# Causal attention by query tiles with streamed keys, and the feed of a finished tile run in half-tile steps between attention blocks

## The chip, the cores and the metric

The kernel runs on one core of one Trainium2 chip. The metric is the time of one execution on the device, in microseconds. The core has TensorE (PE in the profile), VectorE (DVE), ScalarE (ACT), GpSimd (POOL) and SyncE (SP), which here only issues DMAs. Each engine takes its instructions in the order of its own program, and the engines meet in semaphores. An instruction whose semaphore isn't there yet holds up all that stands behind it on its engine.

## The reference

One transformer layer on x of 4096 tokens by 256 channels, 16 heads of 16 channels. Cut to what matters (weights have a low-rank part that is folded in first):

```python
a = lora_linear(layernorm(x), w_attn, ...)            # to q, k, v
att = softmax(causal(q @ k.T / sqrt(16)))             # 16 heads, 4096 x 4096
x = x + layernorm(lora_linear(att @ v, w_proj, ...))
h = layernorm(x)
for blk in range(3):                                  # the feed
    y = qlora(h, 2*blk)                               # 256 -> 256
    y = gelu(layernorm(y) * gamma[blk] + beta[blk], approximate=False)
    h = qlora(y, 2*blk + 1) + h
x = x + layernorm(h)
```

## The kernel before

The program has stages, one after the other, each a block in which all engines start together: `prepare_weights`, `project` (q, k, v of all tokens; q and k go to DRAM in split parts, v stays on chip in `v_all`), `guard` (skipped here: it runs only where scores are large), `attend` and `feed`.

**attend.** The 4096 tokens are 8 tiles of 512. The outer loop (`Fori(0, NG)`, a hardware loop) runs over 4 groups of 4 heads. Its body is written out in full and goes through the query tiles from the last (j=7) to the first (j=0), and for each through its key blocks of 128: first the 4 blocks of the diagonal, with 512, 384, 256 and 128 queries left of 512, then the 4j full ones. That is 144 blocks a group, 576 in all, of which 128 are diagonal (32 sets of 4) and 448 full. For a block, `score` (L761) makes on PE the scores of 2 pairs of heads into `S`, which has 3 places of one pair. ACT takes the exp of each pair (L729) into `probs`, which has 6 places. POOL cuts the triangle in a diagonal block (L702). `weigh` (L779) multiplies the probabilities of four heads side by side with v into `O`, the last row of each head being the sum for the division. PE's order is score(b), weigh(b-2). `score` of pair n waits for the exp of pair n-3, which empties its place, and `weigh(b)` for both exps of b. At the end of a query tile DVE copies `O`, which has two places, into `acc` (L741, L745). Half of the tiles stay on chip, half go to DRAM. The q and k of the whole group (`q_op`, `k_op`) lie on chip. SP loads those of the next group tile by tile (L482, 8 DMAs for q of a tile and 8 for k), behind the tiles that no longer need them. In the first group ACT's queue issues 16 of the k loads.

**feed.** After all of attention it handles the tiles in 2 rounds of 4 at a time ("streams"), in an order that `orders()` works out from a table of durations. Per tile: the sums are turned by PE and divided (L946, L1043, L1044), projected (product L929), normalised and added to x, normalised again, and sent through three blocks of product, normalisation, turn (L922), gelu (L990), product, addition. The normalisation is shared: statistics on DVE (L100 to L110), the inverse root in 10 small steps on POOL (L80 to L90), the scaling on ACT (L977).

## Time and profile before

| what | us |
| --- | --- |
| median of 3 runs | 1530.82 (1530.27 to 1532.49) |
| profiled execution, its own time | 1532.92 |
| its span in the profile | 1531.2 |
| first matmul of attention, from the span's start | 177.29 |
| first matmul of each further head group | 435.99 and twice more, the last group's part ending near 1208 |
| feed | from there to the end |

The profiled execution is 1.7 us longer than its span, and 2.1 us longer than the median. The slices of the span show PE and ACT both at nine tenths or more through attention. In the feed ACT falls to about half and PE stays high. The rows themselves stand in a section of their own below.

### The profile page before, as it was taken

The numbers are of one execution on the slowest core, as the hardware profiler recorded it, in microseconds if no ns is written. First come the engines' busy times: TensorE is split into PE (matmuls) and PEld (weight loads), VectorE is DVE, ScalarE is ACT, GpSimd is POOL, SyncE is SP. The second block draws the span as 40 slices with busy tenths as digits, with TensorE's granted clock in tenths as the row PEclk, the third lists the DMA queues.
The fourth block names the chain that finished last, engine by engine and source line by source line (L and its number), as shares of the span: only waits on it lengthen the run. The fifth ranks groups of instructions, "written<-read, shape, count | busy, mean of one in ns | idle before, by whom it ended". The sixth has DMA issues, their size and how long they took to land. (4 is left out here: it accounts for less than half of the span.)

```text
span 1531.2 us, 27338 instructions
## 1 busy us (share of the span) xinstructions
PE 1415.8 (92%) x8838; PEld 621.7 (41%) x8838; DVE 319.3 (21%) x871; ACT 1218.0 (80%) x1552; POOL 315.9 (21%) x938
## 2 busy tenths in 40 slices
PE   6899499999989999998999998999999879997995
PEld 2455222222322223232223232222232558886784
DVE  3366100000000000000000000000000285578756
ACT  1366399999979999997999998999999555545644
POOL 0121100000120000021000012000010166446754
PEclk7699699999989999998999999999999999998998
...
GB/s 142 60 227 190 140 128 28 29 29 28 49 93 1 28 28 29 29 71 71 24 6 29 29 45 79 45 2 1 1 1 8 129 58 1 1 56 55 1 1 55
DMA packets 60327, 77.62 MB, mean 51 GB/s; under 512 B 16016, under 2 KB 31376, under 8 KB 60176
## 3 DMA queue, kind: packets, MB, share of 16 engines
...
## 5 line engine op out<-in xcount | busy, mean ns | idle before, releaser
L729 ACT ACTIVATE probs<-S 128x1024 f32<-128x1024 f32 (+3 forms) x1152 | 981.3, 1173 | 70.8 <-PE S L761 67.0
L779 PE MATMUL O<-probs,vg 128*32 128x512 f32 (+3 forms) x4608 | 578.8, 575 | 0.6 <-POOL probs L702 0.5
L761 PE MATMUL S<-q_op,k_op 64*128 64x512 f32 (+3 forms) x2304 | 502.4, 480 | 44.4 <-DMA k_op<-qk_rows 17.4
L761 PEld LDWEIGHTS S<-q_op,k_op 64*128 64x128 f32 x2304 | 213.7, 187 | 604.8 <-ACT probs L729 562.3
L702 POOL TENSOR_SCALAR_AFFINE_SELECT probs<-probs 128x256 f32<-128x256 f32 x256 | 102.7, 406 | 928.1 <-ACT probs L729 919.7
L929 PE MATMUL psC<-wfT,yTC 128*128 128x256 f32 x768 | 175.1, 386 | 7.9 <-ACT yTC L990 5.5
L741 DVE COPY acc<-O 128x512 f32 x16 | 11.1, 691 | 777.1 <-PE O L779 777.1
L929 PEld LDWEIGHTS psC<-wfT,yTC 128*128 128x128 f32 x768 | 146.6, 194 | 29.5 <-ACT yTC L990 7.1
L779 PEld LDWEIGHTS O<-probs,vg 128*32 128x32 f32 x4608 | 91.5, 108 | 138.6 <-issue 118.3
L977 ACT ACTIVATE yC<-uC,nmrC,rstdC 128x256 f32<-128x256 f32 x128 | 66.3, 590 | 56.4 <-POOL nmrC L93 56.3
L984 ACT COPY yTC<-psC 128x1024 f32<-128x1024 f32 x32 | 31.6, 1007 | 56.0 <-PE psC L922 56.0
L745 DVE COPY acc<-O 128x512 f32<-128x512 f32 x16 | 11.1, 691 | 248.9 <-PE O L779 248.9
L450 PE MATMUL psQ<-acc,wqkvT 128*128 128x512 f32 x128 | 59.9, 623 | 1.2 <-ACT acc L338 1.2
L1014 POOL TENSOR_TENSOR hbC<-hC,bffn 128x1024 f32<-128x1024 f32 x24 | 57.3, 2397 | 11.8 <-DVE hC L1036 10.6
L354 ACT ACTIVATE qf<-psQ,bqk 128x512 f32<-128x512 f32 x32 | 21.9, 684 | 34.7 <-PE psQ L450 34.2
L990 ACT ACTIVATE yTC<-psC,beta,gamma 128x512 f32<-128x512 f32 x48 | 34.3, 773 | 15.2 <-PE psC L922 15.2
L100 DVE BATCH_NORM_STATS2 stC<-uC 128x6 f32<-128x256 f32 x128 | 45.0, 414 | 1.1
L922 PE MATMUL psC<-ident,yC 128*128 128x128 f32 x256 | 34.4, 282 | 9.0 <-ACT yC L977 8.8
L450 PEld LDWEIGHTS psQ<-acc,wqkvT 128*128 128x128 f32 x128 | 24.8, 199 | 31.6 <-issue 31.6
L1036 DVE TENSOR_TENSOR uC<-psC,bffn 128x1024 f32<-128x1024 f32 x24 | 29.3, 1222 | 39.1 <-PE psC L929 39.1
L1036 DVE TENSOR_TENSOR hC<-psC,hbC 128x1024 f32<-128x1024 f32 x24 | 29.4, 1224 | 34.2 <-PE psC L929 34.0
L929 PE MATMUL psC<-wpT,yTC 128*128 128x256 f32 x128 | 30.9, 398 | 5.7 <-ACT yTC L984 5.7
...
## 6 DMA issues: line engine op xcount, KB each, us to landing
qk_rows<-parts SPq DMA_DIRECT2D x32, 512.0 KB, 3.1
q_op<-qk_rows SPq DMA_DIRECT2D x256, 64.0 KB, 2.3
k_op<-qk_rows SPq DMA_DIRECT2D x240, 64.0 KB, 2.3
...
xC<-in_L_attn_x SPq DMA_DIRECT2D x8, 512.0 KB, 4.8
...
out<-uC SPq DMA_DIRECT2D x8, 512.0 KB, 3.1
acc<-in_L_attn_x ACTq DMA_DIRECT2D x6, 512.0 KB, 4.7
```

Source lines behind the costliest of these rows:

```text
L100: last = nc.vector.bn_stats(st[:, b, :], src[:, b, :])
L450: last_mm = nc.tensor.matmul(psQ[:, m, :], g["wqkvT"][:, c, m * P:(m + 1) * P], xnT[:, u, c, :], start=(c == 0), stop=(c == NC - 1))
L702: nc.gpsimd.affine_select(out=tri, in_=tri, compare_op=ALU.is_ge, fill=0.0, base=0, pattern=[[0, 2], [1, P]], channel_multiplier=-1).then_ ...
L729: nc.scalar.activation(probs[:, pair % NP, :, 0:TT - q0], S[:, pair % NS, :, 0:TT - q0], ACT.Exp, scale=SCALE).then_inc(exp_ok, 1)
L761: last = nc.tensor.matmul(S[:, pair % NS, a, 0:TT - q0], k_op[mine, pair % 2, kb * P:(kb + 1) * P], q_op[mine, pair % 2, j * TT + q0:(j + ...
L779: last = nc.tensor.matmul(O[h * STRIP:(h + 1) * STRIP, o % 2, q0:TT], vg[:, kb, h, :], probs[:, (2 * b + h // 2) % NP, h % 2, 0:TT - q0], ...
L922: last = nc.tensor.transpose(ps[k][:, c * TT + b * P:c * TT + (b + 1) * P], src[:, b, c * P:(c + 1) * P], g["ident"][:, :])
L929: last = nc.tensor.matmul(ps[k][:, b * C:(b + 1) * C], yT[k][:, c, b * P:(b + 1) * P], w[:, c, :], start=(c == 0), stop=(c == NC - 1))
L977: last = nc.scalar.activation(dst[:, b, :], src[:, b, :], ACT.Identity, bias=nmr[k][:, b:b + 1], scale=rstd[k][:, b:b + 1])
L990: last = nc.scalar.activation(yT[k][:, c, :], ps[k][:, c * TT:(c + 1) * TT], ACT.Gelu, bias=g["beta"][:, col:col + 1], scale=g["gamma"][:, ...
L1014: nc.gpsimd.tensor_tensor(hb[k], h[k], repeated(g["bffn"][:, (2 * m + 1) * C:(2 * m + 2) * C]), ALU.add).then_inc(hb_ok[k], 1)
L1036: return nc.vector.tensor_tensor(dst, ps[k][:, :].rearrange("p (b c) -> p b c", b=NB), addend, ALU.add)
```

## The change

The loops of attention are turned round, and `attend` and `feed` become one stage, `attend_and_feed`.

- The outer order is now the query tile t from 0 to 7, and inside it the 4 head groups i. A pair (t, i) is a "visit", 32 in all. There is no hardware loop over groups: all 576 blocks are written out.
- q and k are no longer held for the whole group. Each visit loads its q tile (`q_op`, 3 places), and the k of each 512 keys that it goes through (a "chunk", `k_op`, 8 places). That is 144 chunk loads and 32 q loads of 8 DMAs each, all on SP, each set in a hardware loop of one turn (`Fori(0, 1)`). ACT issues none.
- v is written by `project` straight into the form that `weigh` reads, with the column of ones behind each head, so POOL's copies for each group go.
- `O` has one place. At a visit's end DVE turns it in 32x32 blocks into `o_turned`, divides, turns it back and SP moves the rows into `attT` (4 DMAs a visit). `acc`, its DRAM copy and PE's turning of the sums go.
- The feed of tile t runs in 22 steps on PE (11 steps for each half tile of 256 tokens), each between two blocks of attention: from block 26 + 76t on, about every 3.45 blocks, moved to a visit's end where one is near. All steps go through one PSUM place `F`, and each waits until DVE has emptied it for the step before. The steps of the last tile stand behind all blocks.
- The feed's normalisation is done by DVE alone (inverse root in dependent steps on 128x2 values, scaling too). ACT keeps the gelu, one call for both halves of a tile: 3 a tile, 21 of them between exps and 3 behind them all. The addition of h goes into the product's evacuation, for the last block into PE (4 more products with the identity).

`plan()` lays out all engines' orders with a table of durations when the kernel is built.

```diff
+VD = D + 1
+V_COLS = H * VD + STRIP - VD
...
+                    sp.dma_start(g["b2T"][:, m:m + 1], d["biases"][2 * (m // NC) + 1, at].rearrange("(p o) -> p o", o=1)).then_inc(small_in, 16)
...
-                    nc.gpsimd.memset(g["vg"][:, :, :, D:STRIP], 1.0).then_inc(ones_ok, 1)
-                    pool.wait_ge(ones_ok, 1)
+                    nc.gpsimd.memset(v_heads[:, :, :, D:VD], 1.0).then_inc(ones_ok, 1)
+                    nc.gpsimd.memset(g["vg"][:, :, H * VD:], 1.0).then_inc(ones_ok, 1)
...
-                    nc.vector.tensor_tensor(g["v_all"][:, bass.ds(n * NB, NB), :], psV[:, :, :],
-                                            g["bv"][:, :].unsqueeze(1).to_broadcast([P, NB, C]), ALU.add).then_inc(v_out, 1)
+                    for b in range(NB):
+                        last_v = nc.vector.tensor_tensor(v_heads[:, bass.ds(n * NB + b, 1), :, 0:D].rearrange("p o h e -> p (o h) e"),
+                                                         psV[:, b, :].rearrange("p (h e) -> p h e", e=D),
+                                                         g["bv"][:, :].rearrange("p (h e) -> p h e", e=D), ALU.add)
+                    last_v.then_inc(v_out, 1)
...
+HT = TT // 2
+HB = HT // P
...
+NS, NP = 3, 6
+RING, QS, AS = 8, 3, 3
+VISITS = [(t, i) for t in range(NT) for i in range(NG)]
+CHUNKS = [(v, s) for v, (t, i) in enumerate(VISITS) for s in range(t, -1, -1)]
...
+STEPS = ["project", "turn_x"] + [f"{x}{m}" for m in range(BLK) for x in ("first", "turn", "second")]
+FEED_FROM, FEED_EACH = 26.0, 76.0
...
+    for t in range(NT - 1):
+        for n, (name, k) in enumerate((name, k) for name in STEPS for k in range(2)):
+            at = FEED_FROM + FEED_EACH * (t + n / (2 * len(STEPS)))
+            near = min(boundary, key=lambda b: abs(b - at))
+            at = near if abs(near - at) < 1.7 else int(at)
+            steps.setdefault(at, []).append((name, t, k))
+    pe = []
+    for b in range(NBLK + LAG):
+        if b < NBLK:
+            pe.append(("score", b))
+        if b >= LAG:
+            pe.append(("weigh", b - LAG))
+        pe += steps.get(b, [])
+    pe += [(name, NT - 1, k) for name in STEPS for k in range(2)]
...
+                for x in order["SP"]:
+                    if x[0] == "k_load":
+                        c = x[1]
+                        v, s = CHUNKS[c]
+                        if c >= RING:
+                            sp.wait_ge(scored, 2 * CHUNK_END[c - RING] + 2)
+                        with sp.Fori(0, 1):
+                            load_rows(sp, d, k_op[:, c % RING, :, :], 1, VISITS[v][1], slice(s * TT, (s + 1) * TT), k_in[c % RING], LOW + need)
+                    elif x[0] == "q_load":
+                        v = x[1]
+                        t, i = VISITS[v]
+                        if v >= QS:
+                            sp.wait_ge(scored, 2 * LAST[v - QS] + 2)
+                        with sp.Fori(0, 1):
+                            load_rows(sp, d, q_op[:, v % QS, :, :], 0, i, slice(t * TT, (t + 1) * TT), q_in[v % QS], LOW + need)
...
+                        sp.wait_ge(o_ready, v + 1)
...
+                        for h in range(HG):
+                            row = (i * HG + h) * D
+                            sp.dma_start(attT[row % P:row % P + D, t % AS, row // P, :], o_div[h * STRIP:h * STRIP + D, v % 2, :]).then_inc(
+                                moved[v % 2], 16)
...
+                for _, n in order["POOL"]:
+                    pool.wait_ge(exp_ok, n + 1)
+                    tri = probs[:, n % NP, :, 0:P]
+                    nc.gpsimd.affine_select(out=tri, in_=tri, compare_op=ALU.is_ge, fill=0.0, base=0,
+                                            pattern=[[0, 2], [1, P]], channel_multiplier=-1).then_inc(cut_ok, 1)
...
-                with act.Fori(0, NG) as i:
-                    for b, (o, j, kb, q0) in enumerate(blocks):
...
+                for x in order["ACT"]:
+                    if x[0] == "exp":
...
+                    else:
+                        m, t = int(x[0][-1]), x[1]
+                        for k in range(2):
+                            act.wait_ge(dve_ok[k], done[f"copy{m}", t, k])
+                        for c in range(NC):
+                            col = m * NC + c
+                            last = nc.scalar.activation(zT[:, c, :], zT[:, c, :], ACT.Gelu, bias=g["beta"][:, col:col + 1],
+                                                        scale=g["gamma"][:, col:col + 1])
+                        last.then_inc(gelu_ok, 1)
...
+                def score(b):
+                    v, t, c, kb, q0 = BLOCKS[b]
+                    if b == 0 or BLOCKS[b - 1][0] != v:
+                        pe.wait_ge(q_in[v % QS], LOAD * (v // QS + 1))
+                    if kb % NB == 0:
+                        pe.wait_ge(k_in[c % RING], LOAD * (c // RING + 1))
+                    for n in (2 * b, 2 * b + 1):
+                        if n >= NS:
+                            pe.wait_ge(exp_ok, n - NS + 1)
...
+                def weigh(b):
+                    v, t, c, kb, q0 = BLOCKS[b]
+                    i = VISITS[v][1]
+                    first = kb == t * NB
+                    if first and v:
+                        pe.wait_ge(o_out, v)
...
+                    if b in DIAG:
+                        pe.wait_ge(cut_ok, cuts[2 * b + 1])
+                    for h in range(HG):
+                        col = (i * HG + h) * VD
+                        last = nc.tensor.matmul(O[h * STRIP:(h + 1) * STRIP, q0:TT], vg[:, kb, col:col + STRIP],
+                                                probs[:, (2 * b + h // 2) % NP, h % 2, 0:TT - q0], start=first,
+                                                stop=b == LAST[v], skip_group_check=True)
+                    last.then_inc(pv_ok, 1)
...
+                for x in order["PE"]:
+                    if x[0] == "score":
+                        score(x[1])
+                        continue
+                    if x[0] == "weigh":
+                        weigh(x[1])
+                        continue
+                    name, t, k = x
+                    if place[x]:
+                        pe.wait_ge(f_out, place[x])
...
+                    if name == "project":
+                        for s in range(2):
+                            pe.wait_ge(moved[s], 16 * HG * (2 * t + 2))
+                        last = product(k, lambda c, b: attT[:, t % AS, c, tok(b)], g["wpT"])
+                    elif name.startswith("turn"):
+                        pe.wait_ge(dve_ok[k], done["norm_x" if m is None else f"norm{m}", t, k])
+                        for c in range(NC):
+                            for b in range(HB):
+                                last = nc.tensor.transpose(F[:, c * HT + b * P:c * HT + (b + 1) * P], y[k][:, b, c * P:(c + 1) * P],
+                                                           g["ident"][:, :])
+                    elif name.startswith("first"):
+                        pe.wait_ge(dve_ok[k], done[f"add{m - 1}" if m else "copy_x", t, k])
+                        last = product(k, lambda c, b: hT[k][:, c, b * P:(b + 1) * P], g["wfT"][:, 2 * m])
...
+                    elif m < BLK - 1:
+                        pe.wait_ge(gelu_ok, gelus[f"gelu{m}", t])
+                        for o in range(NC):
+                            for c in range(NC):
+                                last = nc.tensor.matmul(F[:, o * HT:(o + 1) * HT], g["wfT"][:, 2 * m + 1, c, o * P:(o + 1) * P],
+                                                        zT[:, c, k * HT:(k + 1) * HT], start=(c == 0), stop=(c == NC - 1))
...
+                                nc.tensor.matmul(F[:, b * C:(b + 1) * C], zT[:, c, tok(b)], g["wfT"][:, 2 * m + 1, c, :], start=(c == 0),
+                                                 stop=False, skip_group_check=True)
+                            for c in range(NC):
+                                last = nc.tensor.matmul(F[:, b * C + c * P:b * C + (c + 1) * P], hT[k][:, c, b * P:(b + 1) * P],
+                                                        g["ident"][:, :], start=False, stop=(c == NC - 1), skip_group_check=True)
+                    last.then_inc(f_ok[k], 1)
...
-                with dve.Fori(0, NG) as i:
-                    for o in range(NT):
-                        dve.wait_ge(pv_ok, tile_done(i, o))
-                        if o < KEPT:
-                            nc.vector.tensor_copy(g["acc"][o][:, bass.ds(i, 1), :], O[:, o % 2:o % 2 + 1, :]).then_inc(acc_ok, 1)
...
-                with pe.Fori(0, NG) as i:
-                    for b in range(NBLK + LAG):
-                        if b < NBLK:
-                            score(i, b)
-                        if b >= LAG:
-                            weigh(i, b - LAG)
...
+                def normal(k, src):
...
+                    for b in range(HB):
+                        last = nc.vector.bn_stats(st[k][:, b, :], src[:, b, :])
+                    link(k, last)
+                    for b in range(HB):
+                        last = nc.vector.bn_aggr(mv[k][:, b, :], st[k][:, b, :])
+                    link(k, last)
+                    t, v, a, r = tmp[k][:, 0, :], tmp[k][:, 1, :], tmp[k][:, 2, :], rstd[k]
+                    link(k, nc.vector.tensor_scalar(v, mv[k][:, :, 1], EPS, None, ALU.add))
+                    link(k, nc.vector.tensor_scalar(r.bitcast(I32), v.bitcast(I32), -0.5, RSQRT_SEED, ALU.mult, ALU.add))
+                    link(k, nc.vector.tensor_tensor(t, r, r, ALU.mult))
+                    link(k, nc.vector.scalar_tensor_tensor(t, t, -0.5, v, ALU.mult, ALU.mult))
...
+                    link(k, nc.vector.tensor_tensor(t, t, a, ALU.mult))
+                    link(k, nc.vector.scalar_tensor_tensor(r, t, 1.875, r, ALU.add, ALU.mult))
+                    return nc.vector.scalar_tensor_tensor(nmr[k], mv[k][:, :, 0], -1.0, r, ALU.mult, ALU.mult)
...
+                for x in order["DVE"]:
+                    if x[0] == "turn_o":
+                        v = x[1]
+                        dve.wait_ge(pv_ok, LAST[v] + 1)
+                        if v:
+                            dve.wait_ge(o_ready, v)
+                        nc.vector.transpose(o_turned[:, :, :].rearrange("p b e -> p (b e)"), O[:, :]).then_inc(o_out, 1)
+                        continue
+                    if x[0] == "divide":
+                        v = x[1]
+                        dve.wait_ge(o_out, v + 1)
+                        nc.vector.reciprocal(o_rl[:, :], o_turned[:, :, D]).then_inc(o_chain, 1)
+                        dve.wait_ge(o_chain, 2 * v + 1)
+                        nc.vector.tensor_tensor(o_turned[:, :, 0:D], o_turned[:, :, 0:D], bcast(o_rl[:, :], D), ALU.mult).then_inc(o_chain, 1)
+                        dve.wait_ge(o_chain, 2 * v + 2)
+                        if v >= 2:
+                            dve.wait_ge(moved[v % 2], 16 * HG * (v // 2))
+                        nc.vector.transpose(o_div[:, v % 2, :], o_turned[:, :, :].rearrange("p b e -> p (b e)")).then_inc(o_ready, 1)
...
-    d["acc"] = nc.dram_tensor("acc_sums", [NG, NT, P, TT], F32).ap()
...
-            guard(nc, g, d)
-            attend(nc, g, d)
-        feed(nc, g, d)
+        guard(nc, g, d)
+        attend_and_feed(nc, g, d)
```

How the instructions stand now. First PE, at the feed step before a gelu in tile 0 of the feed (attention of tile 2 is running). The names: `S` are scores, `O` is the weighing, `F` the feed's PSUM place. Before, around a diagonal set:

```order
L761 MATMUL S<-q_op,k_op 128x512 x2
L777 REGISTER_ALU
L779 MATMUL O<-probs,vg 32x256 x4
L758 REGISTER_ALU
L761 MATMUL S<-q_op,k_op 128x512 x2
L758 REGISTER_ALU
L761 MATMUL S<-q_op,k_op 128x512 x2
L777 REGISTER_ALU
L779 MATMUL O<-probs,vg 32x128 x4
```

Now, with the turn of half 1 (from `yC1`) that ends the normalised tile, and the product that needs the gelu (from `zT`):

```order
L960 MATMUL F<-ident,yC1 128x128 x4
L913 MATMUL S<-q_op,k_op 128x256 x4
L929 MATMUL O<-probs,vg 32x512 x4
L913 MATMUL S<-q_op,k_op 128x128 x4
L929 MATMUL O<-probs,vg 32x384 x4
L913 MATMUL S<-q_op,k_op 128x512 x4
L929 MATMUL O<-probs,vg 32x256 x4
L913 MATMUL S<-q_op,k_op 128x512 x4
L929 MATMUL O<-probs,vg 32x128 x4
L969 MATMUL F<-zT,wfT 128x256 x4
```

Between the turn and the product stand four blocks' scores and weighings.

Second ACT. Before, the end of the loop over groups, and the feed's first instruction behind it:

```order
L729 ACTIVATE probs<-S 128x2x128
L723 REGISTER_ALU
L723 COMPARE_AND_BRANCH
L657 UNCONDITIONAL_BRANCH
L973 UNCONDITIONAL_BRANCH
L984 COPY yTC<-psC 128x1024 x3
```

Now, at the gelu that belongs to the turn above:

```order
L889 ACTIVATE probs<-S 128x1024 x15
L896 ACT_TABLE_LOAD
L896 ACTIVATE zT<-zT,beta,gamma 128x512 x2
L889 ACT_TABLE_LOAD
L889 ACTIVATE probs<-S 128x1024 x3
L889 ACTIVATE probs<-S 128x2x384 x2
```

The gelu and two loads of a table now stand between exps. ACT's program has 44 table loads, where it had 2.

Third SP, at the start of attention. Before, the q of three tiles, then k and q in turn:

```order
L482 DMA q_op<-qk_rows 16x2x512 x6
L482 ISA
L482 DMA q_op<-qk_rows 16x2x512
L482 ISA
L482 DMA q_op<-qk_rows 16x2x512 x7
```

Now, a chunk, the moves of a finished visit and the begin of a q load:

```order
L839 UNCONDITIONAL_BRANCH
L489 DMA k_op<-qk_rows 16x2x512 x6
L489 ISA
L489 DMA k_op<-qk_rows 16x2x512
L489 ISA
L489 DMA k_op<-qk_rows 16x2x512
L839 REGISTER_ALU
L839 COMPARE_AND_BRANCH
L857 DMA attT<-o_div 16x512 x4
L846 UNCONDITIONAL_BRANCH
L489 DMA q_op<-qk_rows 16x2x512 x6
```

SP's program begins with k, k, q, k, q, k, q, k, the 4 moves of visit 0, q, k. Each set of 8 stands in a loop of its own.

## Rows read from the trace of the kernel before

**Rows 1.** The page: span, and the clock that TensorE was granted, in 40 slices.

```profile
span 1531.2 us, 27338 instructions
PEclk7699699999989999998999999999999999998998
```

**Rows 2.** Groups by line and shape, exps of full blocks: busy, mean, idle before.

```profile
L729 ACT ACTIVATE probs<-S 128x1024 f32<-128x1024 f32 x960 | 883.4, 1252 | 61.6 <-PE S L761 61.6
```

**Rows 3.** Timeline of two steady blocks: start, duration, idle before and its releaser.

```profile
858.45 1.07 PE L779 MATMUL O<-probs,vg 128*32 128x512 f32 x8
859.45 0.19 PEld L761 LDWEIGHTS S<-q_op,k_op 64*128 64x128 f32 x2 [0.84 <-ACT probs L729]
...
859.85 0.19 PEld L761 LDWEIGHTS S<-q_op,k_op 64*128 64x128 f32 x2 [0.22 <-ACT probs L729]
860.28 0.16 PEld L779 LDWEIGHTS O<-probs,vg 128*32 128x32 f32 x8 [0.24 <-issue]
```

**Rows 4.** Timeline of PE over tile j=1 of the first group.

```profile
412.01 0.91 PE L761 MATMUL S<-q_op,k_op 64*128 64x512 f32 x4
...
418.33 0.77 PE L761 MATMUL S<-q_op,k_op 64*128 64x512 f32 x4
419.02 0.64 PE L779 MATMUL O<-probs,vg 128*32 128x256 f32 x8
...
421.88 0.50 PE L761 MATMUL S<-q_op,k_op 64*128 64x512 f32 x2 [0.41 <-ACT probs L729]
...
425.14 0.90 PE L761 MATMUL S<-q_op,k_op 64*128 64x512 f32 x4
```

**Rows 5.** Timeline at a group's end, and the branches that end a turn (ns).

```profile
435.99 1.54 PE L761 MATMUL S<-q_op,k_op 64*128 64x512 f32 x6 [3.44 <-issue]
...
L784 PEldq COMPARE_BRANCH  x4: 79/3548/3761, 432.2 to 1208.0; - x4
...
L673 SPq COMPARE_BRANCH  x3: 40/50/53, 450.1 to 967.6; - x3
```

**Rows 6.** Stretches: length, busy us of PE, PEld, DVE, ACT, POOL, granted clock, DMA.

```profile
436.00:445.70 9.70, 8.90 (x44) 3.28 (x44) 0.00 (x0) 5.75 (x9) 3.20 (x8) 0.50 0.45 130
446.00:456.00 10.00, 9.69 (x72) 3.11 (x72) 0.00 (x0) 10.00 (x12) 0.00 (x0) 1.00 0.25 81
...
954.40:961.10 6.70, 5.91 (x32) 2.02 (x28) 0.00 (x0) 4.98 (x8) 2.78 (x7) 0.50 0.50 139
...
1364.00:1367.30 3.30, 3.30 (x17) 3.07 (x16) 2.50 (x13) 1.75 (x3) 1.38 (x8) 0.50 0.00 0
...
1517.60:1531.00 13.40, 0.00 (x0) 0.00 (x0) 5.02 (x14) 4.15 (x8) 3.50 (x13) 0.50 0.34 117
```

**Rows 7.** Timeline of PE in the feed, a gap ahead of the third stretch above.

```profile
1363.72 1.79 PE L922 MATMUL psC<-ident,yC 128*128 128x128 f32 x8 [1.98 <-ACT yC L977]
```

**Rows 8.** Timeline at the start of attention, SP's queue and PE.

```profile
166.60 11.96 SPq L482 DMA_DIRECT2D q_op<-qk_rows  x24
...
177.29 1.54 PE L761 MATMUL S<-q_op,k_op 64*128 64x512 f32 x6 [17.43 <-DMA k_op<-qk_rows]
```

**Rows 9.** Timeline of PE in the feed: a whole product and a whole turn.

```profile
1413.62 3.62 PE L929 MATMUL psC<-wfT,yTC 128*128 128x256 f32 x16
...
1437.01 1.04 PE L922 MATMUL psC<-ident,hC 128*128 128x128 f32 x8
```

**Rows 10.** Timeline of ACT at the first gelu.

```profile
1261.37 1.28 ACT L990 ACT_TABLE_LOAD   x1
1263.32 1.44 ACT L990 ACTIVATE yTC<-psC,beta,gamma 128x512 f32<-128x512 f32 x2 [0.67 <-PE psC L922]
```

**Rows 11.** Instructions of DVE by line (minimum, median, maximum ns), and the copy's group.

```profile
L104 DVE BATCH_NORM_AGGREGATE mvC<-stC x192: 146/149/183, 1228.6 to 1519.8; 128x2 f32<-128x6 f32 x192
L100 DVE BATCH_NORM_STATS2 stC<-uC x128: 406/409/429, 1227.1 to 1500.5; 128x6 f32<-128x256 f32 x128
...
L110 DVE TENSOR_SCALAR rstdC<-tmpC x48: 169/170/188, 1229.3 to 1520.2; 128x4 int32<-128x4 int32 x48
...
L741 DVE COPY acc<-O 128x512 f32 x16 | 11.1, 691 | 777.1 <-PE O L779 777.1
```

**Rows 12.** The page's DMA issues: count, KB each, median us to landing.

```profile
q_op<-qk_rows SPq DMA_DIRECT2D x256, 64.0 KB, 2.3
...
out<-uC SPq DMA_DIRECT2D x8, 512.0 KB, 3.1
```

638 lines of the change are left out of this document (265 added, 373 removed).

## The prediction, made blind

> **What bounds the kernel now.** I read the page's slices and clock first [rows 1]: PE and ACT are both full through attention, so the question is which of them sets the pace, and by how much. The groups by line give ACT's price: 883.4 us for 960 exps of a full block's pair [rows 2], 0.92 each, 1.83 a block. The timeline of steady blocks shows the same period on PE, from weighing to weighing 1.83 (858.45 to 860.28), and what PE waits for in it: the weights for a block's second pair of scores stand 0.22 behind an exp [rows 3]. So ACT sets the pace in full blocks. PE is close behind. Where it doesn't wait, both pairs of scores take 0.69 (418.33 to 419.02) [rows 4], and weighing to the next score is 1.00 [rows 3], together 1.69. PE has 0.14 us of slack a block, 63 us over 448 full blocks. A query tile costs its full blocks plus a fixed sum for its diagonal set: tile j=1 takes 13.13 (412.01 to 425.14), less 4 x 1.83 is 5.8, of which 0.4 is a visible wait for ACT [rows 4]. So a set needs 5.2 to 5.8 of PE; I take 5.2, since some waits for POOL's triangle stay.
>
> At each group's end PE stands 3.44 for its branch [rows 5], and the clock then is at the lower level (0.50, that is 1.2 GHz) for 9.7 us of work, and 6.7 in the last case [rows 6]. The three turns cost, with these, about 7 each. Then the feed runs alone from near 1208 to 1531, 323 us.
>
> **What the change removes.** The feed's 323 us, and 21 for the three group ends. That is all that it can win: the 576 blocks stay. Against that stand five costs. PE's order is fixed, so I add along PE.
>
> **1. The start.** Before, PE begins at 177.3 with q and k of the tile already queued on two engines [rows 8]. Now SP alone feeds it, and the first visits are short: four diagonal blocks for two loads of 8 DMAs. SP needed 11.96 us for 24 DMAs [rows 8], 4.0 a load, and the loop of one turn adds its branch, 0.05 on SP [rows 5], and some register work: 4.2. Up to the q of tile 2's first visit (visit 8) SP issues 23 loads (96.6), 6 moves of 4 DMAs (24 x 0.47 = 11.4) and 2 loads of x (0.9), and the last lands 2.3 later [rows 12]: 166.6 + 96.6 + 11.4 + 0.9 + 2.3 = 278. PE's own work until there is 8 sets (42), 16 full blocks (27) and 7 feed steps (9), 78 us, so 23 us are lost against a start at 177.3. From tile 2 on a visit has 4 loads and a move (19 us) against 25 and more of PE, and SP gets ahead.
>
> **2. The blocks from there on.** 432 full ones at PE's 1.69: 730. 24 diagonal sets at 5.2: 125.
>
> **3. The feed on PE.** A whole product is 3.62 and a whole turn 1.04 [rows 9]; halves cost half. A tile has 7 products (25.3), 4 turns (4.2), the eight identity products of the last addition (two passes of 0.13 each, 2.1) and 22 changes to and from attention, which I put at 0.1 each from the 0.1 us that weighing needs beyond its streaming (2.2). 33.8 a tile, 237 for seven, less the 9 inside the start: 228. This uses up the slack of 0.14 a block and much more, so PE bounds and ACT has room. ACT's own sum is 432 x 1.83 (791), at most 5.8 a set (139) and the 21 gelus below (84): at most 1014 of some 1240 us.
>
> **4. The gelus.** This is the cost that decides. A gelu takes ACT away for a table load, two calls and a load back: 1.28 + 1.44 + 1.28 = 4.0 [rows 10]. The order puts it behind the exps of the block after the turn. Count from the turn's end. The next scores give ACT its first exp at about 0.6 (an estimate: one pair's scores take half of 0.69, and signals must pass), the two exps of that block end at 2.5, the gelu at 6.5, and the next exp at 7.4. PE in that time scores, weighs, scores, weighs (3.4) and the first pair of the third score (0.3). The second pair needs the place of that next exp. PE stands from 3.7 to 7.4. In 6 of the 21 cases one more exp goes first and the wait is near 3. Mean 3.5, and nothing in PE's queue can pass it: `weigh`, the feed steps and the other scores are all behind. 21 x 3.5 = 74.
>
> And the clock. Each gap of the trace like this was followed by the lower level: 3.44 at a group's end [rows 5, 6], and even 1.98 in the feed [rows 6, 7]. After 3.44 it lasted 9.7 us of work. Before, that cost only 2 us at a group's begin, since the short blocks there waited for ACT anyhow. Now PE is the bound and half speed for 7 to 10 us costs 3.5 to 5, and at least the 1.2 to 2 seen. I take 3.5: another 74. Together 147.
>
> The same outage has a price on a page alone: the Trainium skill, "ScalarE: Activation LUTs", section "What ACT_TABLE_LOAD costs", has a drain of about 1.38 us beside each load. No row shows it, as the one gelu behind a load waited for PE [rows 10]. By it the outage is 2.8 longer, and an estimate of the total is 58 us higher, 1694.
>
> **5. Handing over O, and DVE.** With one place for `O`, the first weighing of a visit waits for DVE's turn. No row shows that turn: a copy of the same tile is 0.69 [rows 11], half or double of it are the bounds. In its shadow PE has a score (0.56 to 0.7) and at 28 of 32 ends a feed step, so 8 us in all, 0 to 30. DVE's work, an estimate of 65 us a tile (ten normalisations of 3.3, as in 6, and as much again in evacuations, copies and scalings), lies beside 170 and more of PE.
>
> **The end of the last visit** then is 278 + 730 + 125 + 228 + 147 + 8 = 1516.
>
> **6. The last tile's feed** has nothing beside it. Per half, a normalisation on DVE is two statistics (0.41), two aggregations (0.15) and eleven dependent small steps at 0.17 [rows 11] plus a gap, 0.2: 3.3. A half tile's evacuation is taken as the copy's 0.69 [rows 11] and a gap, 0.8 to 0.9, a half product as 1.9. Along the longer of DVE and PE: divide and move 6.6. Projection, both normalisations of both halves, turn, copy 22.5. Three times product, evacuation, normalisation and scaling of both halves, turns and copies, 13.2 each, 39.6. Two times gelu, product, add, product, add (1.6 + 1.9 + 0.9 + 1.9 + 0.9), 14.4, since one `F` lets the second product start only after the first add. Gelu, last products, normalisation and result of both halves 15.2. Store 3.1 [rows 12] and the end 0.5. Sum 102. PE is idle for most of each normalisation, so the clock is at 1.2 GHz as in the last 13.4 us of the trace [rows 6], and about 20 us of products on this path double: 18 more. 120.
>
> **Sum.** Span 1516 + 120 = 1636. The profiled execution is 1.7 above its span and 2.1 above the median, so the median is the span less 0.4: 1636, 7% slower.
>
> **The rivals.**
>
> A, the sum above: 1600 to 1690, by 1.66 to 1.75 a block, 5 to 9 a gelu.
>
> B, the gelu waits stand but the clock doesn't fall: against it is every gap of 2 us and more that I found, for it that those came with other gaps around. 1636 - 74 - 18 = 1544, still 13 us slower, since start (23), table switches (74) and the serial last tile (102) eat what overlap gives.
>
> C, faster: PE has work in ACT's outage, because in the real run ACT and PE drift so that a feed product (1.8) falls into most of them, and turns and gelus find ACT with nothing due. Then both gelu terms go: 1544 - 74 = 1470. It turns faster when a gelu costs PE under 2.8 us with its clock effect. Against it: the program's order puts the next product three to four blocks behind the turn, beyond the place where PE stops, and orders can't drift on an engine.
>
> D, SP becomes the bound: a loop of one turn costs what PE's branch costs (3.5) and not SP's 0.05 [rows 5]. SP would need 176 x 7.5 + 160 x 0.47 = 1395, from 166.6 on, and the end is 1562 + 120 = 1682, with the gelu waits hidden in it. The row of SP itself speaks against it. The Trainium skill, "Advanced Engine Details and Errata", section "Control Flow Timing", has 108 ns for a compare-and-branch, an estimate of 10 us more on SP and none on PE.
>
> E, DVE meets a visit's end inside a normalisation and PE waits 3.3 more at half of the ends, with the clock's fall: 16 x 6.9 = 110, toward 1740. DVE's order puts the turn ahead of such pieces by plan, and the real PE is later than planned, not earlier.
>
> **How the numbers follow.** A 0.55, B 0.22, C 0.10, D 0.06, E 0.07. A measurement of this kernel can tell about 0.2% (3 us) from no change. Faster by more than that is C and a sliver of B: 0.11. Within it 0.02, also out of B. Slower 0.87. The range takes in A and B with D: 1540 to 1695.
>
> **What would show it.** In the new profile: PE's first score of visit 8 near 278. Full blocks at 1.69 and no longer at 1.83 between steps. PE gaps of 3 to 4 us on `S`, released by the exp behind each table load, 21 of them, with the clock at 0.50 behind them. ACT idle for some 150 to 200 us. From the last weighing to the end 120 us with the clock at 0.50. I am wrong if the blocks run at 1.83 beside the steps, if gaps at gelus are under 2 us, if SP has no idle time in the middle, or if the clock stays at 1.00 behind a gap of 3 us.

## The result

| | kernel before | changed kernel |
| --- | --- | --- |
| median (lowest to highest), us | 1531.65 (1530.27 to 1533.18) | 1650.33 (1644.27 to 1651.27) |
| profiled execution, its span | 1532.92, 1531.2 | 1650.64, 1648.9 |

The ratio is 1.0766, 95% interval 1.0738 to 1.0795: the changed kernel is 7.7% slower. Predicted were 1636 us with a range of 1540 to 1695.

The page of the changed kernel answers to [rows 1]. The lines are its span, the two slices of busy tenths, the clock, and from its costliest groups the exps and the table loads:

```profile
span 1648.9 us, 26922 instructions
...
PE   6898478999989998998999989989899999989344
...
ACT  1464356888788877887888868888878888889010
...
PEclk7799679999999999999999999999999999999667
...
L889 ACT ACTIVATE probs<-S 128x1024 f32<-128x1024 f32 (+3 forms) x1152 | 996.8, 980 | 287.2 <-PE S L913 285.3
...
L896 ACT ACT_TABLE_LOAD x22 | 28.2, 1283 | 51.6 <-DVEq L1058 51.3
```

ACT has fallen to eight tenths and PE is the engine that is full. The waits (engine, what it waited for, from whom: total, times, longest) show that PE nevertheless still waits for ACT, and how long one such wait can be:

```profile
PEld S L913 <- ACT probs L889: 352.4, 388, 4.6
```

The reason is in the timeline around a gelu (start, duration, engine, line, in brackets idle time before and who ended it):

```profile
392.84 0.66 PE L960 MATMUL F<-ident,yC 128*128 128x128 f32 x4
...
395.05 1.28 ACT L896 ACT_TABLE_LOAD   x1
...
395.75 1.06 PE L929 MATMUL O<-probs,vg 128*32 128x512 f32 x8
396.34 1.52 ACT L896 ACTIVATE zT<-zT,beta,gamma 128x512 f32<-128x512 f32 x2
397.88 1.28 ACT L889 ACT_TABLE_LOAD   x1
399.17 4.69 ACT L889 ACTIVATE probs<-S 128x1024 f32<-128x1024 f32 x5
...
400.25 1.71 PE L913 MATMUL S<-q_op,k_op 64*128 64x512 f32 x4 [3.44 <-ACT probs L889]
...
403.75 0.50 PEld L913 LDWEIGHTS S<-q_op,k_op 64*128 64x128 f32 x4 [1.66 <-ACT probs L889]
```

ACT is away from its exps for 4.1 us (395.05 to 399.17). PE scores and weighs two more blocks behind its turn, until 396.81, and then stands 3.44. There are 21 such gaps, 3.01 to 4.32 long, 74.5 us in all. The stretches around this one (length, busy us of PE, PEld, DVE, ACT, POOL, clock, DMA):

```profile
396.80:400.00 3.20, 0.01 (x2) 0.00 (x0) 0.00 (x0) 3.17 (x4) 0.00 (x0) 1.00 0.24 60
400.00:406.80 6.80, 6.43 (x25) 1.51 (x25) 0.00 (x0) 5.80 (x7) 0.00 (x0) 0.50 0.08 18
407.00:413.80 6.80, 6.80 (x45) 4.08 (x45) 1.56 (x3) 3.35 (x4) 1.47 (x4) 1.00 0.50 134
```

Behind the gap the granted clock is 0.50, that is 1.2 GHz, for 6.8 us, and then 1.00 again. Between the first score of visit 8 and the last weighing the clock was at 0.50 in 24 stretches, 136.5 us, and one of them begins within 1.5 us of the end of each of the 21 gaps.

### The profile page after: what moved, and what is told of

The parts are those of the page before. It is cut to its first block, busy times and chain, and to the rows that moved or that the text cites. A ratio compares the mean times of both kernels' runs of the same rounds, so it can differ in the third digit from the quotient of the medians.

```text
span 1648.9 us, 26922 instructions
## 1 busy us (share of the span) xinstructions
PE 1410.6 (86%) x8646; PEld 585.4 (36%) x8646; DVE 638.4 (39%) x2232; ACT 1162.1 (70%) x1370; POOL 134.2 (8%) x355
## 4 chain that ended last, share of the span: by engine, by line
PE 66%; DVE 9%; ACT 8%; issue 4%; SPq 3%; DMA 0%; DVEq 0%; ACTq 0%
PE O L929 29%; PE S L913 20%; PE F L937 7%; PE F L969 5%; ACT probs L889 5%; SPq L489 3%; PE F L975 2%; PE F L960 2%; ACT L889 2%; ACT zT L896 1%; DVE stC L998 1%; DVE yC L1018 1%; PE F L978 1%; DVE uC L1050 1%; SPq L857 1%
## 5 line engine op out<-in xcount | busy, mean ns | idle before, releaser
L913 PE MATMUL S<-q_op,k_op 64*128 64x512 f32 (+3 forms) x2304 | 449.4, 459 | 119.6 <-ACT probs L889 81.1
L1050 DVE TENSOR_TENSOR uC<-F,bffn 128x512 f32<-128x512 f32 x64 | 44.0, 687 | 275.9 <-PE F L937 152.5
L937 PE MATMUL F<-wfT,hT 128*128 128x256 f32 x384 | 99.3, 403 | 6.2 <-DVEq L1051 3.1
L960 PE MATMUL F<-ident,yC 128*128 128x128 f32 x256 | 44.5, 300 | 54.3 <-DVE yC L1018 54.3
L937 PEld LDWEIGHTS F<-wfT,hT 128*128 128x128 f32 x384 | 71.2, 195 | 50.1 <-issue 32.6
L969 PE MATMUL F<-zT,wfT 128*128 128x256 f32 x256 | 80.6, 469 | 8.9 <-ACT zT L896 6.7
L969 PEld LDWEIGHTS F<-zT,wfT 128*128 128x128 f32 x256 | 57.6, 237 | 50.3 <-issue 38.0
L896 ACT ACTIVATE zT<-zT,beta,gamma 128x512 f32<-128x512 f32 x48 | 36.4, 805 | 47.6 <-DVEq L1058 47.3
L1018 DVE TENSOR_SCALAR yC<-uC,rstdC,nmrC 128x256 f32<-128x256 f32 x160 | 59.1, 412 | 7.6 <-DVE uC L1050 2.5
L457 PE MATMUL psQ<-xnT,wqkvT 128*128 128x512 f32 x128 | 59.3, 618 | 1.2 <-ACT xnT L341 1.2
```

Of the source, the lines that this page charges most:

```text
L457: last_mm = nc.tensor.matmul(psQ[:, m, :], g["wqkvT"][:, c, m * P:(m + 1) * P], xnT[:, u, c, :], start=(c == 0), stop=(c == NC - 1))
L896: last = nc.scalar.activation(zT[:, c, :], zT[:, c, :], ACT.Gelu, bias=g["beta"][:, col:col + 1], scale=g["gamma"][:, col:col + 1])
L913: last = nc.tensor.matmul(S[:, n % NS, a, 0:TT - q0], k_op[mine, c % RING, n % 2, kb % NB * P:(kb % NB + 1) * P], q_op[mine, v % QS, n % 2 ...
L937: last = nc.tensor.matmul(F[:, b * C:(b + 1) * C], src(c, b), w[:, c, :], start=(c == 0), stop=(c == NC - 1))
L960: last = nc.tensor.transpose(F[:, c * HT + b * P:c * HT + (b + 1) * P], y[k][:, b, c * P:(c + 1) * P], g["ident"][:, :])
L969: last = nc.tensor.matmul(F[:, o * HT:(o + 1) * HT], g["wfT"][:, 2 * m + 1, c, o * P:(o + 1) * P], zT[:, c, k * HT:(k + 1) * HT], start=(c ...
```

## The experiments

"Last weighing" is its end, "middle" the time from visit 8's first score to there. "Low" is how long the clock was at 0.50 in the middle, "tail" what follows the last weighing. The spans of one profiled execution each; the medians have their ratios to the kernel before.

| kernel | median | ratio, 95% | visit 8 | last weighing | middle | low | tail |
| --- | --- | --- | --- | --- | --- | --- | --- |
| changed | 1650.33 | 1.0766 (1.0738 to 1.0795) | 295.4 | 1527.1 | 1231.7 | 136.5 | 121.8 |
| e1, no table loads | 1551.5 | 1.0134 (1.0105 to 1.0163) | 294.9 | 1430.6 | 1135.7 | 27.3 | 118.8 |
| e2, no gelu | 1518.5 | 0.9918 (0.989 to 0.9947) | 295.0 | 1401.5 | 1106.5 | 20.5 | 115.1 |
| e3, fill | 1614.9 | 1.0548 (1.0517 to 1.0578) | 295.9 | 1488.9 | 1193.0 | 23.9 | 124.6 |
| e4, feed from 36 | 1653.0 | 1.0797 (1.0765 to 1.0828) | 295.6 | 1531.7 | 1236.1 | 125.4 | 119.4 |
| e5, two places | 1641.1 | 1.0699 (1.0676 to 1.0722) | 295.9 | 1527.6 | 1231.7 | 136.5 | 113.0 |
| e6, padded | 1628.9 | 1.0623 (1.0605 to 1.0641) | 283.8 | 1502.7 | 1218.9 | 112.6 | 124.6 |
| e7, tanh | 1552.5 | 1.0133 (1.0116 to 1.0151) | 293.9 | 1425.1 | 1131.2 | 17.1 | 124.4 |
| e8, e5 to e7 together | 1537.3 | 1.0028 (1.0019 to 1.0038) | 282.2 | 1420.9 | 1138.8 | 23.9 | 113.7 |
| e9, e8 and the table | 1514.2 | 0.988 (0.9864 to 0.9897) | 283.5 | 1399.2 | 1115.7 | 3.4 | 114.2 |
| e10, e9 and q on ACT | 1501.1 | 0.9792 (0.9776 to 0.9808) | 270.9 | 1386.6 | 1115.7 | 3.4 | 114.4 |
| e11, e10 and split | 1514.5 | 0.9887 (0.9871 to 0.9904) | 275.5 | 1398.7 | 1123.2 | 3.4 | 113.2 |
| e12, e10 and gelu | 1599.1 | 1.0434 (1.0417 to 1.0451) | 272.3 | 1484.5 | 1212.2 | 109.2 | 113.0 |

### What a gelu costs: e1, e2 and e3

e1 leaves out the gelu's function (another stands in its place) and e2 the whole gelu, so neither is a kernel to use: they price it. e3 computes all that the changed kernel does.

```diff
-last = nc.scalar.activation(zT[:, c, :], zT[:, c, :], ACT.Gelu, bias=...
+last = nc.scalar.activation(zT[:, c, :], zT[:, c, :], ACT.Identity, bias=...
```

> The 24 gelus become calls of Identity with the same scale and bias, so this leaves out the gelu's function, and the two table loads around each go. ACT is then away for 1.5 us instead of 4.1. Theory A (each table switch makes PE stand and lets its clock fall): the 21 gaps of 3.5 us on the scores shrink to under 1.3, the stretches at 0.50 between tile 2 and the last weighing go from 24 to 5 or fewer, and the time falls by 54 (gaps) and 50 to 65 (clock), to about 1535 to 1550. Theory B (the gaps cost only themselves, the lower clock is hidden behind ACT): 54 less, about 1596. Theory C (the gaps are hidden by what ACT would be behind with anyway): under 20 less.

```diff
-for c in range(NC):
-    last = nc.scalar.activation(zT[:, c, :], zT[:, c, :], ACT.Gelu, ...)
-last.then_inc(gelu_ok, 1)
+act.sem_inc(gelu_ok, 1)
```

> ACT's gelu calls are left out altogether (the products then read the normalised tile), so ACT is away for nothing. Against the run with Identity this prices ACT's own 1.5 us a call. Theory A: PE never waits for it in either, so 0 to 5 us less than there from attention, and 3 x 1.5 = 5 from the last tile's chain. A theory in which ACT's sum of work counts (ACT as the bound) would give 24 x 1.5 = 36 less.

```diff
 for x in order["PE"]:
     if x[0] == "score":
+        if x[1] in fills:       # 3 blocks behind turn{m} of half 1, tiles 0 to 6
+            pe.wait_ge(f_out, fills[x[1]])
+            for _ in range(7):
+                nc.tensor.matmul(F[:, 0:C], g["wfT"][:, 0, 0, 0:P], g["wfT"][:, 0, 0, :], start=True, stop=True)
         score(x[1])
```

> Nothing is left out. In each of the 21 gaps PE makes 7 products of 128x256 on constant data into the empty place F (about 3.0 us), right ahead of the score that waits. PE isn't done earlier by that, only busy. If the lower clock behind the gaps costs what the sum says (theory A), the stretches at 0.50 go and the time falls by 45 to 70. If the clock costs nothing (theory B), the time stays or rises by up to 10.

e1 gave 1551.5, just above the 1535 to 1550 expected. Without the table loads 99 us are gone: the two loads (2.6 us) are the larger part of an outage, all 21 gaps of 3 us and more went with them, and the stretches at 0.50 fell from 24 to 5. e3 keeps every wait of the engines on each other and only gives PE something to do in it:

```profile
391.72 1.52 ACT L896 ACTIVATE zT<-zT,beta,gamma 128x512 f32<-128x512 f32 x2
392.12 3.29 PE L950 MATMUL F<-wfT 128*128 128x256 f32 x14
393.25 1.28 ACT L889 ACT_TABLE_LOAD   x1
...
395.62 0.49 PE L913 MATMUL S<-q_op,k_op 64*128 64x512 f32 x2 [0.21 <-ACT probs L889]
```

The low clock fell from 136.5 to 23.9 us, and the time by 35.5, less than the 45 to 70 expected. From the score ahead of a gelu's last turn to the score 14 blocks on, the 21 gelus sum to 746.9 us in the changed kernel, 704.4 in e3, 648.9 in e1, 618.9 in e2. So a gelu costs (746.9 - 618.9) / 21 = 6.1 us: its two table loads with all that follows from them 4.7, its calls 1.4. Cut the other way, the clock is (746.9 - 704.4) / 21 = 2.0 of it and the gap 3.5. The 0.5 left over I put down to smaller waits behind the gap; it wasn't measured by itself.

The gelus alone decide the sign: without them (e2) the new order takes 1518.5, 13 us less than the kernel before.

e2 is 33 less than e1 where 5 to 10 were expected. That is a miss, and a lesson. A call of 1.5 us without any table load still cost 29 / 21 = 1.4 in the middle. The explanation offered is ACT's row above, 5 exps in 4.69: with the last at 1.06, one starts every 0.91, 1.82 a block. PE needs 1.66. So between two products ACT is the slower engine, and the products (2.0 of PE each) are what gives it its time back. Around a gelu there are only turns, of 0.66, for ten blocks. ACT is free for 30% of the span, but not there. e11 below tests this.

### The start and DVE's order: e4, e6

```diff
-FEED_FROM, FEED_EACH = 26.0, 76.0
+FEED_FROM, FEED_EACH = 36.0, 76.0
```

> The feed begins 10 blocks later (FEED_FROM 36 for 26), nothing else. In the changed kernel PE stood 8.1 us in the start at the first turn, waiting for DVE's two normalisations, with a stretch at 0.50 behind it. Theory: in the start SP sets the pace and the feed step came too early for DVE; later, a step comes every 7 us and DVE keeps up, so that gap goes and the first score of visit 8 comes at about 282 instead of 295. The 7 steps that stood there for nothing (9 us) must be done later. Net 3 to 8 us faster. If the start is bound by SP alone, no change or slower.

It gave 1653.0 where 3 to 8 us less than 1650.3 were expected, and visit 8 began at 295.6 as before and not at 282. That is a miss. What stood in the way is in the changed kernel's rows:

```profile
260.58 3.70 SPq L489 DMA_DIRECT2D q_op<-qk_rows  x8
...
264.54 7.66 SPq L489 DMA_DIRECT2D k_op<-qk_rows  x16
265.94 1.37 DVE L1018 TENSOR_SCALAR yC<-xC,rstdC,nmrC 128x256 f32<-128x256 f32 x4
...
266.81 1.09 PE L960 MATMUL F<-ident,yC 128*128 128x128 f32 x4 [8.09 <-DVE yC L1018]
...
274.95 3.88 SPq L489 DMA_DIRECT2D q_op<-qk_rows  x8
...
295.41 0.73 PE L913 MATMUL S<-q_op,k_op 64*128 64x512 f32 x4
```

SP had issued visit 8's q from 274.95 on, but PE was late itself. It had stood 8.1 us ahead of the first `turn_x`, since DVE had not scaled x yet. Moving the feed by ten blocks moved this wait along with it: e4 has gaps of 3.70 and 2.73 ahead of the two turns, and 1.65 at `O`.

```diff
+SLOTS = STEPS[:1] + [""] + STEPS[1:]
-FEED_FROM, FEED_EACH = 26.0, 76.0
+FEED_FROM, FEED_EACH = 26.0, 78.0
...
-            at = FEED_FROM + FEED_EACH * (t + n / (2 * len(STEPS)))
+            if not name:
+                continue
+            at = FEED_FROM + FEED_EACH * (t + n / (2 * len(SLOTS)))
```

> An empty pair of slots is put between the projection's two halves and turn_x (24 slots a tile in place of 22, and a tile's feed spreads over 78 blocks in place of 76, so that neighbouring steps stand 3.25 blocks apart and not 3.45). Nothing is left out. Theory G: PE came to turn_x too early, since DVE needs 2 x 9.8 us for evacuation, two normalisations, addition and scaling of two halves, where the slots give it some 3.45 blocks (5.7 us) a step. The gaps of 8.06 (at 258.7), 4.40 and 3.21 before line 960 go, with the slow clock behind each: 15.7 of gaps and about 4 of clock, less the new slots' nothing: 1630 to 1640. Rival: what PE gains there it loses again, since at 258.7 it ran ahead of SP's loads (visit 8's q is issued at 274.95) and DVE's share moves to a later step; under 5 us, 1645 to 1652. The first score of visit 8 tells them apart at the first tile: 285 to 288 by G, 295 by the rival.

1628.9, and visit 8 at 283.8, each 1 us below what theory G gave: it holds. Two slots more between projection and turn give DVE its time, and 21 us are gone, 12 of them before visit 8. The gaps of 8.09, 4.43 and 3.24 ahead of the turns went. One before a weighing did not: it is 4.12 at 1146.7, where the changed kernel has 5.93 at another visit's end.

### The tail: e5

```diff
+def f_of(t, k):
+    return S[:, 0, 0, :] if t == NT - 1 and k else F[:, :]
...
-if place[x]:
+if place[x] and (t < NT - 1 or (name, k) == ("project", 0)):
     pe.wait_ge(f_out, place[x])
```

> Only the last tile's feed changes: half 1 uses a bank of S (no exp is left then) in place of F, so that a step of one half no longer waits for DVE to empty the other half's. Nothing is left out. Attention is untouched, so the last weighing still ends near 1527. Theory F (one place for two halves costs in the serial tail): of the 121.8 us behind the last weighing DVE works 61.8 and PE 49.8, so there is room to overlap; each of 22 steps waits up to one evacuation (0.8) and half a product, and some of these waits lie beside DVE's other work: 8 to 12 us less, 1639 to 1643, ratio to the kernel before 1.070 to 1.073. Rival (the tail is a chain of DVE's dependent small steps, which two places don't shorten): under 3 us, 1648 to 1651.

1641.1, inside theory F's 1639 to 1643; the tail went from 121.8 to 113.0, 8.8 less. The kernels with the gelu in the last tile and one place have tails of 119.4 to 124.6, those with two 113.0 to 114.4. One place for two halves did cost there. The stretches behind the last weighing, first of the changed kernel, then of e5 (columns as above):

```profile
1527.10:1648.90 121.80, 49.67 (x164) 35.47 (x160) 61.81 (x238) 5.83 (x7) 0.00 (x0) 0.68 0.02 6
```

```profile
1527.50:1640.60 113.10, 45.40 (x164) 35.49 (x160) 61.66 (x238) 5.83 (x7) 0.00 (x0) 0.68 0.02 6
```

DVE's work is the same, and the time in which neither works fell only from 23.3 to 21.1: the rest of the gain is time in which PE worked alone.

### Gelu without the table: e7

The change in words, with the arithmetic of each part (`w` is a new tile, `wT` in the rows):

```diff
-gelu{m} on ACT: 2 calls of Gelu for both halves
+copy{m} on DVE, per half: z = F*gamma/2 + beta/2;  w = (z*z + 5.591)*z
+tanh{m} on ACT, per half: w = tanh(0.28542*w), 128x512
+post{m} on DVE, per half: z = (w + 1)*z
```

> For the first seven tiles the gelu is computed by its tanh form, and by halves: copy on VectorE applies half of gamma and beta, then squares and multiplies (2 more operations of 128x512), ScalarE makes one tanh of 128x512 with the table that exp uses (if it needs another, this shows as table loads), and VectorE multiplies once more. The last tile keeps the gelu instruction. Nothing is left out; the gelu of seven tiles is the tanh approximation. Theory A (what costs is the length of ACT's outage at one place, most of all the two table loads): 42 outages of about 0.55 instead of 21 of 4.1; an outage under 0.6 is inside PE's reserve of half a block's pair of scores, so no gap over 1 on S is left beside steps, no low clock behind them, and attention ends as without any gelu: last weighing 1400 to 1412, span 1522 to 1534, ratio 0.995 to 1.003. Rival H (DVE): VectorE gets some 80 us more work in 42 longer chains, PE comes to turns and second products too early and waits there as it did at turn_x, 2 to 4 us at several of the 42: 1550 to 1590. Rival: tanh has its own table, and 42 outages of 3.1 make 1700 and more.

The tanh form approximates the gelu, which the reference asks for exactly, so e7 to e11 do not compute quite the same function as the changed kernel.

1552.5, above theory A's 1534 and inside rival H's 1550 to 1590, though not for H's reason. The tanh needed no table of its own, one load is left for the last tile. All 21 long gaps went, but the last weighing ended at 1425 and not by 1412. The timeline around two tanhs (here of e10, which has the same form) shows why:

```profile
366.92 0.63 ACT L914 ACTIVATE wT<-wT 128x512 f32<-128x512 f32 x1 [0.27 <-DVE wT L1097]
...
368.51 0.49 PE L937 MATMUL S<-q_op,k_op 64*128 64x512 f32 x2 [0.56 <-ACT probs L908]
...
373.31 0.63 ACT L914 ACTIVATE wT<-wT 128x512 f32<-128x512 f32 x1 [0.27 <-DVE wT L1097]
...
374.90 0.44 PE L937 MATMUL S<-q_op,k_op 64*128 64x384 f32 x2 [0.62 <-ACT probs L908]
```

A call of 0.63 can make PE wait 0.56. It is e2's lesson again: e7's last weighing is 23.6 later than e2's, 0.56 for each of 42 tanhs in the mean. Not each tanh shows such a wait. Waits of PE on scores of 0.2 and more are 36 in e7's middle (21.0 us) and 10 in e2's (4.2), which is 17 of the 24; the rest was not found. There was no "reserve of half a block's scores". The two longest waits for DVE, H's reason, are 5.92 and 4.41 in e7, but e2 has them as well (5.92 and 4.43), so VectorE's added work did not bring them.

### Together, and a better plan: e8 and e9

> All three together: tanh form by halves for the first seven tiles, the empty pair of slots ahead of turn_x with 78 blocks a tile, two places for the last tile's feed. Nothing is left out. If the three are independent, it is the tanh kernel less 15 to 20 at turn_x and less 8 to 12 in the tail: 1495 to 1510, ratio 0.977 to 0.986, faster than both kernels. By rival H (DVE too late for steps that stand closer together) it loses at second products what it gains at turn_x: 1530 to 1560.

1537.3, where 1495 to 1510 were expected; it lies in the 1530 to 1560 of rival H. The tail kept its gain (113.7) and so did the start (282.2), but the middle is 7.6 longer than in e7. PE did wait for DVE, only not at the second products, where H had it: at three visits' ends it stood 5.45, 7.17 and 4.32 before the first weighing. The second of them in e8:

```profile
748.64 0.69 DVE L1078 TENSOR_TENSOR uC<-F,bproj 128x512 f32<-128x512 f32 x1 [1.60 <-PE F L961]
...
749.57 0.75 DVE L1023 BATCH_NORM_STATS2 stC<-xC 128x6 f32<-128x256 f32 x2 [0.24 <-DVE uC L1078]
...
753.09 0.74 DVE L1023 BATCH_NORM_STATS2 stC<-uC 128x6 f32<-128x256 f32 x2
...
758.22 0.71 DVE L1055 STREAM_TRANSPOSE o_turned<-O 128x512 f32<-128x512 f32 x1
...
758.99 1.93 PE L947 MATMUL O<-probs,vg 128*32 128x512 f32 x8 [7.17 <-DVE o_turned L1055]
```

Two normalisations, with their scalings and an addition, stand ahead of the turn of `O`, which PE's last weighing had left ready some 7 us earlier. The plan has a normalisation at 3.3 us, where the first here takes from 749.57 to 753.09, 3.5, without its scaling.

```diff
-("ln_x", "DVE", 3.3, ...), ("norm_x", "DVE", 0.5, ...), ("turn_x", "PE", 0.6, ...), ("copy_x", "DVE", 0.75, ...)
+("ln_x", "DVE", 3.65, ...), ("norm_x", "DVE", 0.85, ...), ("turn_x", "PE", 0.7, ...), ("copy_x", "DVE", 0.95, ...)
...
-    for _ in range(3):
+    for _ in range(10):
...
-item(("turn_o", v), "DVE", 0.8, [("weigh", LAST[v])], LAST[v])
+item(("turn_o", v), "DVE", 0.8, [("weigh", LAST[v]), ("divide", v - 1) if v else None], LAST[v])
```

> The kernel with the tanh form, padded slots and two places in the tail, and only the table of durations from which DVE's order is planned changed to what the traces show (normalisation 3.65 in place of 3.3, scaling 0.85 for 0.5, evacuation 0.95 for 0.75, addition of x 1.55 for 1.2, product 1.95 for 1.8, a load 3.95 for 3.6), with 10 passes of the plan in place of 3, and a turn of O never planned ahead of the division before it. PE's order and the work are the same, nothing is left out. Theory J (the waits of 5.44, 7.17, 4.32 and 1.85 before the first weighing of a visit are DVE's order: a normalisation stands ahead of the turn of O because the plan has it shorter than it is): they go, with some 5 us of low clock: 12 to 22 less, 1515 to 1525, ratio 0.989 to 0.995. Rival: the order is tight everywhere, and the waits move to other visit ends or to turns: within 5 us of 1537.

1514.2, 1 us below theory J's 1515 to 1525. The same visit end in e9:

```profile
742.81 0.72 DVE L1055 STREAM_TRANSPOSE o_turned<-O 128x512 f32<-128x512 f32 x1 [1.09 <-PE O L947]
...
743.58 1.07 PE L947 MATMUL O<-probs,vg 128*32 128x512 f32 x8 [0.40 <-DVE o_turned L1055]
744.34 0.94 DVE L1043 TENSOR_SCALAR yC<-xC,rstdC,nmrC 128x256 f32<-128x256 f32 x2 [0.24 <-DVE uC L1078]
```

No gap of 2 us is left between visit 8 and the last weighing. Durations, passes and the added dependency were changed together; which of the three did most was not told apart, nor what SP's order, which the same plan makes, had to do with it.

### The loads at the start: e10

```diff
+if x[0] == "q_load":    # on ACT's queue for the first 3 visits
+    load_rows(act, d, q_op[:, v % QS, :, :], 0, i, slice(t * TT, (t + 1) * TT), q_in[v % QS], LOW + need)
...
-item(("q_load", v), "SP", 3.95,
+item(("q_load", v), "ACT" if v < QS else "SP", 3.95,
```

> As the kernel with the corrected table, and ScalarE's queue issues the first three loads of q (24 DMAs) at the start, while SP issues those of k. Nothing is left out. Theory K (SP's issuing sets the first eight visits: 282 at the first score of visit 8 against a start at 181): SP has 12 us less to issue, the first score comes 4 earlier, at 177, and visit 8 starts 8 to 12 earlier, at 270 to 274; the end moves by the same: 1505 to 1515, ratio 0.981 to 0.988. Rival: these visits wait for DVE's and ACT's share, not for SP: less than 4 us.

```profile
164.57 11.61 ACTq L489 DMA_DIRECT2D q_op<-qk_rows  x23
164.66 11.23 SPq L489 DMA_DIRECT2D k_op<-qk_rows  x22
174.99 1.22 PE L937 MATMUL S<-q_op,k_op 64*128 64x512 f32 x4 [17.26 <-DMA q_op<-qk_rows]
...
207.24 1.22 PE L937 MATMUL S<-q_op,k_op 64*128 64x512 f32 x4 [6.05 <-DMA q_op<-qk_rows]
```

1501.1, 13 less than e9 and below theory K's 1505 to 1515: the first score at 175.0, visit 8 at 270.9, 12.6 earlier than in e9. This is the fastest kernel, 2.1% below the kernel before. With DVE's wait gone it was SP that bound the start, as the prediction had it: even here PE waits 6.05 for a load of q.

### Where it did not help: e11, and the gelu put back: e12

```diff
+steps.setdefault(at, []).append(("open", (name, t, k)))      # first half of the product
+steps.setdefault(at + 1, []).append((name, t, k))            # second half, one block on
```

> As the kernel with q on ScalarE's queue, and each product step of a half is split in two, the second half of its matmuls one block later. The sum of the work is the same, nothing is left out. Theory L (between products ACT is the longer of the two: 0.91 an exp, 1.82 a block against PE's 1.66; a tanh of 0.64 adds to it at the place where only a turn of 0.66 gives it time, so each of the 42 costs a wait of 0.56 in spite of ACT's 30% idle time): pieces of 0.9 us of PE work spread more evenly give ACT its time back before the next tanh. The waits of 0.56 behind line scores fall from some 40 to under 20, 10 to 20 us less, minus up to 0.07 for each of 98 more changes (7): 3 to 13 less than the kernel before it. Rival (the wait comes with each tanh wherever PE's steps are): all of some 40 waits stay, and the changes make it 3 to 8 slower.

1514.5, 13 slower, where theory L had 3 to 13 less and its rival 3 to 8 more. PE's waits of 0.45 to 0.7 ahead of scores fell from 26 to 16 and from 14.8 to 8.9 us. New waits for the feed came, 2.04 ahead of a turn and twice 0.68 ahead of a projection, and all of PE's waits over 0.1 in the middle went only from 24.9 to 21.7. Yet the middle grew by 7.5. If the 98 further changes between attention and feed are what took the rest, they cost (7.5 + 3.2) / 98 = 0.11 each, not 0.07; no run shows this by itself. Visit 8 came 4.6 later. Theory L is right in its direction and not worth its price: more than half of the waits stayed.

> The fastest kernel so far (1501: tanh form, padded slots, corrected table, two places in the tail, q on ScalarE's queue) with one thing put back: the gelus of the first seven tiles are again two calls of the gelu instruction for both halves, with their table loads. Nothing is left out. If an outage of 4.1 us at one place costs 6.1 us wherever it stands (3.5 of gap, 2.0 of low clock, 0.5 of catching up), as measured in the changed kernel, attention grows by 21 x 6.1 = 128 and loses the 24 us of waits at the 42 tanhs: 1501 + 104 = 1605 (1598 to 1612), ratio 1.047, with 21 gaps of 3 to 4.3 and some 20 stretches at 0.50 between visit 8 and the last weighing. Rival (part of the 6.1 came from DVE's order, the early start or F, all mended here): under 4.5 a gelu, below 1575.

1599.1: 98 more, and inside the 1598 to 1612 expected. The middle grew by 96.5, and with the 22.5 of small waits on scores that e10 has there this is (96.5 + 22.5) / 21 = 5.7 a gelu, near the 6.1 and well above the rival's 4.5. The 21 gaps are back, with the clock at 0.50 for 109 us. One of them:

```profile
338.27 1.28 ACT L901 ACT_TABLE_LOAD   x1
...
340.64 1.71 PE L925 MATMUL S<-q_op,k_op 64*128 64x512 f32 x4 [4.32 <-ACT probs L901]
```

## Why the prediction was right, step by step

The sign, the cause and the size held: rival A at 1636, measured 1650.3. The cause is shown (e1 to e3, e12). That the total is off by only 14 is in part luck: the start, the changes to the feed, `O` with DVE and the tail came out some 40 us longer than their terms, the gelus and the blocks 32 shorter. Step by step against the profiled execution:

- **The bound.** Right that PE takes over. Its block was put at 1.69 from [rows 3, 4] and is 1.66 in the median, 13 us less over 432 blocks.
- **The start.** Visit 8 predicted at 278, measured 295.4: the one step whose mechanism was incomplete. SP's part was nearly right: its 23 loads and 6 moves were issued by 278.8 (the last row of 3.88 from 274.95), where the sum has 275.5. DVE's part was missing. "DVE's work lies beside PE's" was said of sums (65 a tile beside 170), and here the place counted: PE's order had `turn_x` before DVE could be ready, 8.1 of gap and the low clock behind it. e6 shows 12 us of it; its 283.8 leaves 6 for the rest.
- **The feed on PE.** A half product adds 2.0, not 1.9, and a turn 0.66 (0.62). 98 products make 10 us.
- **The gelus.** The gap was put at 3.5 and is 3.55 in the mean, 21 times. The clock was put at 3.5 a gelu and e3 measures 2.0. Each low stretch lasts 3.4 to 6.8, but in part of it PE waits for ACT in any case, which is catching up: the weights at 403.75 stood 1.66 behind an exp, at half speed. With 0.5 of smaller waits the term is 128 in place of 147. So it was over-sized by 19, which hid a part of the other misses.
- **O and DVE.** Put at 8. The gaps before weighing and turns in the middle are 5.93, 4.43 and 3.24, and an estimate with the clock behind each is 18. The 5.93 is rival E in a small form, and e9 mends such gaps by DVE's order in a kernel where they were worse. The other two went in e6, when the turns were moved back.
- **The end.** The middle was predicted as 1238 and is 1231.7, by errors of both signs. The start's 17 us late and the middle's 6 short make 1527 in place of 1516.
- **The tail.** 120 predicted, 121.8 measured, with the clock higher than thought (0.68), so that the 18 set down for it were in part something else, which wasn't taken apart.
- **The page's price.** The Trainium skill, "ScalarE: Activation LUTs", section "What ACT_TABLE_LOAD costs", would have put a drain of 1.38 us beside each load and the time at 1694. In the row at 396.34 the gelu follows its load at once, and the outage is 4.1 without any drain. The measurement decides: the changed kernel's 1650.3 is 44 below that estimate.

The rivals: B (the clock doesn't fall) is refuted by the row at 400.00 and by e3. C (work falls into the outages) by 21 gaps of 21. D (SP's loop costs 3.5) by SP's row of 16 DMAs and the loop's branch between them in 7.66. E in its full size (16 long waits for DVE) is refuted by the one of 5.93. Of the marks named, three missed: visit 8, the clock in the tail (0.68 in the mean, not 0.50), and ACT's idle time in the middle, 1231 - 1013 = 218 where 150 to 200 were named. The others showed, but for three of the 21 gaps, which are 4.3 and not 3 to 4.
